# A CIN kernel: chunk 0 in single tiles, W1 in two loads, another order for V and R, and chunk 5's fields behind the stores

## What is computed

```python
X0 = inputs.reshape(-1, 32, 64); Xi = X0; pools = []
for W, b in ((W1, b1), (W2, b2), (W3, b3)):
    Wr = W.reshape(128, 32, Xi.shape[1])
    Xi = jnp.einsum('bhd,bmd,ohm->bod', X0, Xi, Wr) + b[None, :, None]
    pools.append(Xi.sum(axis=-1))
return jnp.concatenate(pools, axis=-1) @ fc_W.T + fc_b
```

## Time and profile before

| what | value |
|---|---|
| three runs | 77.54, 78.10, 78.97 us, median 78.1 |
| the profiled execution | 78.03 us, span 76.2 us, granted TensorE clock 1.00 |
| busy of the span | TensorE 92%, VectorE 66%, ScalarE 49%, GpSimd 46% |
| DMA | 14.10 MB, mean 185 GB/s |

### The profile page before, as it was taken

How to read it: one execution, slowest core, us unless ns; L and a number is a source line. 1 busy time by engine, 2 the same in 40 slices (tenths; PEclk the granted TensorE clock), 3 DMA queues, 4 the chain that set the end, 5 groups by cost and what they waited for, 6 DMA issues and landing times.

```text
span 76.2 us, 1113 instructions
## 1 busy us (share of the span) xinstructions
PE 69.8 (92%) x353; PEld 48.7 (64%) x353; DVE 50.1 (66%) x53; ACT 37.7 (49%) x57; POOL 35.1 (46%) x40
## 2 busy tenths in 40 slices
PE   3999279999899999879999999999999999999970
PEld 1335057666432588568887888888888888877750
DVE  1035999997489888999968497999691300303541
ACT  3720895999799999915767229600760021000000
POOL 4924164992488401910001920999999530053200
DMA  0899999999999999345149997000000000000000
GB/s 11 237 302 241 364 374 361 350 371 388 391 430 386 431 402 354 122 124 154 32 133 421 389 307 297 17 0 0 0 0 0 4 0 0 9 0 0 0 0 0
DMA packets 7337, 14.10 MB, mean 185 GB/s; under 512 B 771, under 2 KB 3907, under 8 KB 6819
## 3 DMA queue, kind: packets, MB, share of 16 engines
q1 hardware_dynamic: 6995, 13.78, 51.3%
q10 hardware_dynamic: 336, 0.25, 1.2%
HBM read 12.98 MB, written 1.05 MB: 184 GB/s over the span
## 4 chain that ended last, share of the span: by engine, by line
PE 72%; ACT 12%; DVE 10%; issue 3%; DVEq 0%
PE a_ps L627 29%; PE x_ps L627 21%; PE x_ps L611 5%; ACT feat L351 5%; PE z_ps L621 4%; ACT zz L351 3%; PE a_ps L713 3%; ACT x L365 3%; PE a_ps L689 2%; PE a_ps L688 2%; DVE z_ps L477 2%; PE x_ps L662 2%; ACT at_sb L351 2%; DVE feat L484 2%; DVE products_of L477 2%
## 5 line engine op out<-in xcount | busy, mean ns | idle before, releaser
L627 PE MATMUL x_ps<-feat,w_hi 128*128 128x512 f32 x64 | 19.3, 402 | 2.7 <-ACT feat L351 1.8
L268 POOL TENSOR_TENSOR xs<-x_in,xs 32x512 fp32r<-32x512 f32 x7 | 9.0, 1285 | 15.9 <-ACT xs L351 14.6
L351 ACT ACTIVATE feat<-z_ps 128x1024 fp32r<-128x1024 f32 x12 | 12.0, 1019 | 8.4 <-POOL xsum L338 5.0
L627 PE MATMUL a_ps<-feat,a_hi 128*128 128x512 f32 x64 | 16.1, 394 | 0.0
L627 PEld LDWEIGHTS x_ps<-feat,w_hi 128*128 128x128 f32 x64 | 11.5, 189 | 6.6 <-issue 3.3
L627 PEld LDWEIGHTS a_ps<-feat,a_hi 128*128 128x128 f32 x64 | 12.0, 188 | 2.8
L275 POOL TENSOR_TENSOR feat<-products_of,feat 128x1024 fp32r<-128x1024 f32 x4 | 9.5, 2387 | 7.9 <-DVE z_ps L477 4.7
L527 DVE SCALAR_TENSOR_TENSOR x<-a_ps,vec,x 128x512 f32<-128x512 f32 x7 | 5.2, 748 | 11.3 <-PE a_ps L689 11.3
L282 POOL TENSOR_TENSOR x<-x 128x512 f32<-128x512 f32 x6 | 7.8, 1292 | 8.1 <-DVE x L527 7.8
L477 DVE TENSOR_TENSOR z_ps<-x_in,r_in 128x1024 f32<-128x1024 f32 x8 | 10.8, 1380 | 0.4 <-DVE products_of L477 0.2
L484 DVE TENSOR_TENSOR feat<-z_ps,feat 128x1024 fp32r<-128x1024 f32 x8 | 9.7, 1222 | 1.7 <-ACT feat L351 1.6
(11 more groups left out here) (69 smaller groups left out, 69.7 us busy)
## 6 DMA issues: line engine op xcount, KB each, us to landing
w_sb<-w SPq DMA_DIRECT2D x9, 512.0 KB, 8.8
r_in<-xr SPq DMA_DIRECT2D x4, 1024.0 KB, 11.5
x_in<-xl SPq DMA_DIRECT2D x8, 256.0 KB, 6.1
a_by_fields<-at_sb SPq DMA_DIRECT2D x4, 192.0 KB, 4.2
x<-x_pairs SPq DMA_DIRECT2D x1, 512.0 KB, 6.5
x<-x SPq DMA_DIRECT2D x1, 512.0 KB, 5.6
w_sb<-w SPq DMA_DIRECT2D x1, 256.0 KB, 6.8
a_by_fields<-at_sb SPq DMA_DIRECT2D x2, 128.0 KB, 4.5
```

The costliest lines, as they stand in the source:

```text
L268: nc.gpsimd.tensor_tensor(xs[rows, c, :], x_in[rows, c % X_BUFS, :], xs[rows, c, :].bitcast(f32), ALU.subtract).then_inc(xs_lo, 1)
L351: return nc.scalar.activation(dst, src, ACT.Copy)
L627: nc.tensor.matmul(bank, weights[:, k, :], feat[:, c, part, k, :], start=(start and k == 0), stop=False)
```

## The change

- SP: W1's four main tiles come in two loads, `w1_first_in` and `w1_in`, with `load_x(1)` between; W1's rest is loaded before `x_pairs`; the right fields of chunk 5 are issued behind the six stores, not ahead of them.
- GpSimd sums W1's main tiles in two halves. ScalarE rounds them in two halves (`main_hi`), and rounds the rest earlier.
- Chunk 0, half 0: `first_mult` multiplies tile by tile, `first_hi_parts` rounds tile by tile.
- VectorE: W1's low part stands behind `lo(0)` and W1's rest sum; `pairs_lo(0)` to `(3)` come earlier; of A, `main_lo` stands ahead of the rest's sum.
- TensorE: other order of `pick_right`, layer 1's pieces, V's parts and R's rounds: V in two stretches (two parts each, as before, at other places), R in two stretches with `x1_lo(1, 1)` between.
- ScalarE: other order of `hi`, `save_a`, `save_x1`, `pairs_hi` and the copy of q.

The diff (blank lines and part of the indentation left out):

```diff
@@ -133,6 +133,7 @@
+w1_first_in = sem("w1_first_in")
@@ -140,6 +141,7 @@
+first_picked, first_z, first_hi = sem("first_picked"), sem("first_z"), sem("first_hi")
@@ -211,11 +213,12 @@
-    sp.dma_start(w1_sb[:, :, 0:TILES, :], w1[:, :, 0:TILES, :]).then_inc(w1_in, 16)
+    sp.dma_start(w1_sb[:, :, 0:PER_HALF, :], w1[:, :, 0:PER_HALF, :]).then_inc(w1_first_in, 16)
 ...
+    sp.dma_start(w1_sb[:, :, PER_HALF:TILES, :], w1[:, :, PER_HALF:TILES, :]).then_inc(w1_in, 16)
 ...
+    sp.dma_start(w1_sb[:, :, EVEN:, :], w1[:, :, EVEN:, :]).then_inc(w1_rest_in, 16)
 ...
-    sp.dma_start(w1_sb[:, :, EVEN:, :], w1[:, :, EVEN:, :]).then_inc(w1_rest_in, 16)
@@ -228,13 +231,13 @@
     load_right(PICKED)
     load_x(4)
     load_x(5)
-    load_right(PICKED + 1)
     sp.dma_start(fcb_sb[:, :], fc_b).then_inc(fcb_in, 16)
     for t in range(0, ROUNDS, 2):
         sp.wait_ge(a_saved, t + 2)
         store_a(EXT, 0, t, 0)
         store_a(EXT, 1, t, HALF)
         store_a(H, 0, t, H)
+    load_right(PICKED + 1)
     load_x(6)
     sp.wait_ge(zeros_done, ZEROS)
     sp.wait_ge(a_out, A_OUT)
@@ -301,11 +304,12 @@
-    pool.wait_ge(w1_in, 16)
-    nc.gpsimd.tensor_tensor(w1_sb[:, 0, 0:TILES, :], w1_sb[:, 0, 0:TILES, :], w1_sb[:, 1, 0:TILES, :],
-                            ALU.add).then_inc(w_sum, 1)
+    for half, landed in enumerate((w1_first_in, w1_in)):
+        pool.wait_ge(landed, 16)
+        nc.gpsimd.tensor_tensor(w1_sb[:, 0, of_half(half), :], w1_sb[:, 0, of_half(half), :],
+                                w1_sb[:, 1, of_half(half), :], ALU.add).then_inc(w_sum, 1)
 ...
-    pool.wait_ge(w_sum, 1)
+    pool.wait_ge(w_sum, 2)
@@ -360,6 +364,14 @@
+    def first_hi_parts(k):
+        if k == 0:
+            act.wait_ge(first_z, 1)
+        else:
+            act.wait_ge(z_done, 1)
+        copy(feat[:, 0, 0, k, :], field_bank(0, 0)[:, k, :]).then_inc(first_hi if k == 0 else hi_done, 1)
@@ -368,6 +380,11 @@
+    def main_hi(half):
+        act.wait_ge(w_sum, half + 1)
+        copy(w1_hi[:, of_half(half), :], w1_sb[:, 0, of_half(half), :]).then_inc(w_hi_done, 1)
@@ -379,23 +396,25 @@
     shifted = bass.AP(pick32[:, :].tensor, 0, [list(pick32[:, :].ap[0]), [1, TILES], [TILES, J], [1, H]])
     copy(pick[:, :, :].rearrange("p k (j h) -> p k j h", j=J), shifted).then_inc(pick_done, 1)
     split_x(0)
-    act.wait_ge(w_sum, 1)
-    copy(w1_hi[:, 0:TILES, :], w1_sb[:, 0, 0:TILES, :]).then_inc(w_hi_done, 1)
-    hi(0, 0)
+    first_hi_parts(0)
     split_x(1)
+    first_hi_parts(1)
+    main_hi(0)
+    split_x(2)
+    main_hi(1)
     hi(0, 1)
-    split_x(2)
     act.wait_ge(z16_done, 1)
     copy(z16_hi[:, :], x16[:, 0, :]).then_inc(hi16_done, 1)
     pairs_hi(0, 0)
+    pairs_hi(0, 1)
     hi(1, 0)
-    pairs_hi(0, 1)
+    hi(1, 1)
+    act.wait_ge(w_rest_sum, 1)
+    copy(w1_hi[:, EVEN:, :], w1_sb[:, 0, EVEN:, :]).then_inc(w_hi_done, 1)
     split_x(3)
     pairs_hi(1, 0)
-    hi(1, 1)
     pairs_hi(1, 1)
-    act.wait_ge(w_rest_sum, 1)
-    copy(w1_hi[:, EVEN:, :], w1_sb[:, 0, EVEN:, :]).then_inc(w_hi_done, 1)
+    hi(2, 0)
     act.wait_ge(vt_ready, 1)
     copy(vt_sb[:, :], vt_ps).then_inc(vt_saved, 1)
     act.wait_ge(v_ready, 1)
@@ -404,26 +423,27 @@
     copy(v_st[:, 0:H].rearrange("o (g c) -> o g c", g=4), v_by_field).then_inc(v_saved, 1)
     copy(v_st[:, H:H + 8], v_by_field[:, 0, :]).then_inc(v_saved, 1)
     copy(v_st[:, H + 8:H + 15], v_by_field[:, 1, 0:7]).then_inc(v_saved, 1)
+    hi(2, 1)
     act.wait_ge(vec_in, 16)
+    save_x1(0)
+    hi(3, 0)
+    save_a(0)
+    save_a(1)
     act.wait_ge(v_saved, 1)
     copy(v_rep[:, :, :], v_st[:, 0:H].rearrange("o (h r) -> o h r", r=1).to_broadcast(
         [P, H, 4])).then_inc(v_saved, 1)
-    hi(2, 0)
-    hi(2, 1)
-    save_a(0)
-    hi(3, 0)
-    save_a(1)
-    save_x1(0)
+    hi(3, 1)
     save_a(2)
     pairs_hi(2, 0)
     save_a(3)
+    save_x1(1)
     pairs_hi(2, 1)
     pairs_hi(3, 0)
-    save_x1(1)
-    hi(3, 1)
+    pairs_hi(3, 1)
+    act.wait_ge(q_ready, 1)
+    copy(q_sb[:, :], q_ps).then_inc(q_saved, 1)
     hi(4, 0)
     hi(4, 1)
-    pairs_hi(3, 1)
     save_x1(2)
     act.wait_ge(zeros_done, ZEROS)
     act.wait_ge(a_out, A_OUT)
@@ -434,18 +454,16 @@
     hi(5, 0)
     save_x1(3)
     hi(5, 1)
+    save_x1(4)
     act.wait_ge(f_sum, 1)
     copy(a_hi[:, 0:TILES, :], f1[:, 0:TILES, :]).then_inc(a_hi_done, 1)
-    save_x1(4)
-    act.wait_ge(q_ready, 1)
-    copy(q_sb[:, :], q_ps).then_inc(q_saved, 1)
     act.wait_ge(f_sum, 2)
     copy(a_hi[0:TERMS, TILES:, :], f1[0:TERMS, TILES:, :]).then_inc(a_hi_done, 1)
     split_x(4)
     split_x(5)
-    save_x1(5)
     hi(6, 0)
     split_x(6)
+    save_x1(5)
     hi(6, 1)
     split_x(7)
     hi(7, 0)
@@ -480,6 +498,8 @@
+        if c == 0:
+            dve.wait_ge(first_hi, 1)
@@ -527,18 +547,28 @@
+    def first_mult():
+        for k in range(PER_HALF):
+            if k == 0:
+                dve.wait_ge(first_picked, 1)
+            else:
+                dve.wait_ge(picked, 1)
+            nc.vector.tensor_tensor(field_bank(0, 0)[:, k, :], x_in[:, 0, :], field_bank(0, 0)[:, k, :],
+                                    ALU.mult).then_inc(first_z if k == 0 else z_done, 1)
 ...
-    mult(0, 0)
+    first_mult()
 ...
-    dve.wait_ge(w_hi_done, 1)
-    main_lo(w1_sb[:, 0, :, :], w1_hi, w1_lo, w_lo_done)
 ...
+    dve.wait_ge(w_hi_done, 2)
+    main_lo(w1_sb[:, 0, :, :], w1_hi, w1_lo, w_lo_done)
@@ -546,32 +576,32 @@
     lo(1)
     mult(2, 0)
     mult(2, 1)
-    dve.wait_ge(w_hi_done, 2)
+    pairs_lo(0)
+    dve.wait_ge(w_hi_done, 3)
     rest_lo(w1_sb[:, 0, :, :], w1_hi, w_lo_done)
-    pairs_lo(0)
+    lo(2)
     mult(3, 0)
+    mult(3, 1)
     pairs_lo(1)
-    lo(2)
+    pairs_lo(2)
     lo(3)
-    pairs_lo(2)
-    mult(3, 1)
+    pairs_lo(3)
     mult(4, 0)
     mult(4, 1)
     lo(4)
     second_lo(4)
     mult(5, 0)
-    pairs_lo(3)
     mult(5, 1)
     lo(5)
     dve.wait_ge(f_main_in, F_MAIN)
     nc.vector.tensor_tensor(f1[:, 0:TILES, :], f1[:, 0:TILES, :], f2[:, 0:TILES, :], ALU.add).then_inc(f_sum, 1)
     second_lo(5)
+    dve.wait_ge(f_sum, 1)
+    dve.wait_ge(a_hi_done, 1)
+    main_lo(f1, a_hi, a_lo, a_lo_done)
     dve.wait_ge(f_rest_in, F_REST)
     nc.vector.tensor_tensor(f1[0:TERMS, EVEN:LIN, :], f1[0:TERMS, EVEN:LIN, :], f2[0:TERMS, EVEN:, :],
                             ALU.add).then_inc(f_sum, 1)
-    dve.wait_ge(f_sum, 1)
-    dve.wait_ge(a_hi_done, 1)
-    main_lo(f1, a_hi, a_lo, a_lo_done)
     dve.wait_ge(f_sum, 2)
     dve.wait_ge(a_hi_done, 2)
     rest_lo(f1, a_hi, a_lo_done)
@@ -620,6 +650,8 @@
+            if c == 0 and half == 0 and k == 0:
+                last.then_inc(first_picked, 1)
@@ -631,7 +663,9 @@
-        pe.wait_ge(w_hi_done, 1)
+        pe.wait_ge(w_hi_done, half + 1)
+        if c == 0 and half == 0:
+            pe.wait_ge(first_hi, 1)
@@ -657,7 +691,7 @@
-        pe.wait_ge(w_hi_done, 2)
+        pe.wait_ge(w_hi_done, 3)
@@ -720,59 +754,51 @@
     pick_right(0, 0)
     pick_right(0, 1)
     keep_clock(5)
-    x1_hi(0, 0)
-    x1_main(0, 1)
+    x1_main(0, 0)
     pick_right(1, 0)
-    x1_low_weights(0, 1)
+    pick_right(1, 1)
+    x1_low_weights(0, 0)
+    x1_hi(0, 1)
     x1_lo(0, 0)
-    pick_right(1, 1)
     v_part(0)
     v_part(1)
-    x1_main(1, 0)
     pick_right(2, 0)
-    x1_low_weights(1, 0)
+    x1_hi(1, 0)
     pick_right(2, 1)
+    x1_lo(1, 0)
+    x1_lo(0, 1)
     v_part(2)
     v_part(3)
-    x1_lo(1, 0)
-    x1_main(1, 1)
+    pick_right(3, 0)
+    x1_tail(0)
     pe.wait_ge(ident_done, 2)
     pe.wait_ge(vt_saved, 1)
     nc.tensor.transpose(v_ps, vt_sb[:, :], ident[:, :]).then_inc(v_ready, 1)
-    x1_lo(0, 1)
-    x1_tail(0)
-    pick_right(3, 0)
+    x1_hi(1, 1)
+    pick_right(3, 1)
     a_round(0)
-    x1_low_weights(1, 1)
     a_round(1)
+    x1_lo(1, 1)
     a_round(2)
     a_round(3)
-    pick_right(3, 1)
-    x1_lo(1, 1)
     x1_tail(1)
-    x1_main(2, 0)
-    x1_low_weights(2, 0)
+    x1_hi(2, 0)
     x1_lo(2, 0)
-    x1_main(2, 1)
-    x1_low_weights(2, 1)
-    x1_main(3, 0)
-    x1_low_weights(3, 0)
-    x1_lo(2, 1)
-    x1_tail(2)
+    x1_hi(2, 1)
     pe.wait_ge(v_saved, 4)
     pe.wait_ge(a_saved, ROUNDS)
     nc.tensor.matmul(q_ps, v_rep[:, :, :].rearrange("p h r -> p (h r)"), vec[:, 1:2],
                      start=True, stop=True).then_inc(q_ready, 1)
+    x1_hi(3, 0)
+    x1_lo(2, 1)
+    x1_tail(2)
     x1_lo(3, 0)
-    x1_main(3, 1)
-    x1_main(4, 0)
-    x1_low_weights(4, 0)
-    x1_low_weights(3, 1)
+    x1_hi(3, 1)
+    x1_hi(4, 0)
+    x1_lo(4, 0)
     x1_lo(3, 1)
-    x1_lo(4, 0)
-    x1_main(4, 1)
     x1_tail(3)
-    x1_low_weights(4, 1)
+    x1_hi(4, 1)
     x1_lo(4, 1)
     x1_tail(4)
     x1_hi(5, 0)
```

## The result

The change makes the kernel slower: 80.09 us (median of four executions, 79.59 to 81.86) against 78.03 us, ratio 1.026 with the interval [1.016, 1.037]: it is slower, while whether by more than 2% is open. The profiled execution took 79.79 us, span 78.0. I had forecast 76.6. Executions more than 1.5% above the fastest of the same kernel are left out of every ratio and interval.

A forecast was written before the change was run, and what follows sets the result against it. TensorE, unbroken from 39.30 to 72.70 us, was bound by the A product's start; 1.28 us earlier plus the 0.24 us stall gave 1.5 us together, so 76.6 us against the 78.1 median, range 75.6 to 78.3.

The forecast's parts named there:

- S: Time at which chunk 5's fields land, when `mult(5,0)` can start: forecast 32.7 us, issue at 27.8 plus about 4.9.
- the rival "slower": Chunk 5's fields land late; at 8.2 us latency the A product starts at 40.95: 79.4 us, chance 0.12.
- The formula from S: Chain from the landing of chunk 5's fields through `lo(5)`, `f_sum` and `a_hi`: A product 4.95 us after the landing.
- 1.5 us: Whole forecast gain: 1.28 us from an earlier A product, plus the 0.24 us stall removed.
- 38.05: Forecast start in us of chunk 0's A product, 39.33 before: 1.28 us gained.
- the 0.24 us stall: TensorE's wait before `a_lo` inside the A product, forecast to vanish because `main_lo` now precedes the late `f_rest` sum.
- the last reloads of A: Reloads ahead of the A product, forecast to land by 35.3 us, before `f_sum` at 36.2.
- the collision: At the front, GpSimd's `split_x(1)` overlapping VectorE's `rest_sum`: a 0.15 us slip would cost 0.6 us.
- a wall: W3's last quarter, landing at 17.0 us before V's last two parts: nothing at the front moves V by more than 0.3 us.
- the front's 0.76 us: First feature matmul on TensorE at 8.9 us in place of 9.66: 0.76 gained, not kept whole.

The follow-up runs named there:

- fields ahead of the stores: Changed kernel with chunk 5's fields issued right behind the fourth `save_a`, ahead of the last three stores: ratio 1.026 to the kernel before, median 80.13 us.
- fields alone: Changed kernel with `load_x(6)` behind the reloads of A, and both queues waiting for chunk 5's fields before issuing reloads: 80.23 us, read for the landing only.
- the fields back: Changed kernel with chunk 5's fields issued at their old place, ahead of the stores: ratio 1.004 to the kernel before, median 78.57 us.
- the last run: Changed kernel with chunk 5's fields in halves, first A product's last two matmuls later, `save_x1(3)` before `hi(5, 0)`, `load_x(6)` behind reloads: ratio 0.992, median 77.34 us.
- the run with the fields between the stores: Changed kernel with chunk 5's fields issued behind the first three stores and ahead of the last three: ratio 1.042 to the kernel before, median 81.0 us.

## Why the prediction was wrong

**The step that failed** is the landing of chunk 5's fields: "The nearest row is chunk 6's fields, 4.9 us from issue to landing on a short queue: 32.7 us." The issue came as forecast (27.91, forecast 27.8), the landing took 7.84 us, and S was 35.75, not 32.7. The place, the wait and the point from which it decides (S above 34.4) stood in the rival "slower", whose 8.2 us and 79.4 us come near the 7.84 and 80.09 measured; I gave it 0.12, because I took a queue that has run out for a fast queue. The rates around it show the opposite (windows view of the kernel after; last two columns: DMA share, GB/s):

```profile
29.00:30.00 1.00, 1.00 (x6) 0.83 (x5) 0.44 (x1) 0.97 (x3) 0.48 (x1) 1.00 0.74 156
30.00:31.00 1.00, 1.00 (x6) 0.82 (x5) 0.69 (x1) 1.00 (x2) 1.00 (x1) 1.00 0.71 205
...
32.00:33.00 1.00, 1.00 (x5) 0.82 (x6) 0.66 (x1) 0.00 (x0) 0.00 (x0) 1.00 0.95 379
```

From 29 to 31 us the DMA engines are busy for 0.7 of the time and move 156 and 205 GB/s. The single packets of the trace, those of 8 KB, in which the fields come:

```
kernel, load               packets   first begins    first packets take     then
before, chunk 5 (full)       128     behind chunk 4  0.31 to 0.34 us        0.31 us
before, chunk 6              128     38.96 us        0.87 to 1.01 (five)    mostly 0.31 us
after, chunk 5               128     29.15 us        0.47 to 1.48 (17)      mostly 0.31 us
fields ahead of the stores   128     27.32 us        1.43 to 1.62 (eight)   mostly 0.31 us
```

A load that is issued when little is left in the queue begins 1.0 to 1.3 us after its issue, and its first packets take up to five times as long as the rest. A load that stands behind others in a full queue has no slow packets, and its start is hidden. Chunk 6's fields in the kernel before have both; their 4.9 us contain it. The three parts of a landing, with what else went through the DMA engines meanwhile, from the same packets:

```
kernel, load               to the first  first packet to  to the    other data
                           packet        end of the last  landing   meanwhile
before, chunk 6            1.15 us       3.36 us          0.4 us    0.12 MB
fields alone, chunk 5      1.30 us       4.63 us          0.4 us    0.03 MB
after, chunk 5             1.24 us       5.86 us          0.7 us    0.56 MB
```

The wait ahead of the first packet is about the same in all three. What grew is the middle: by 1.3 us with nothing behind the load, and by as much again with `load_x(6)` and the reloads in the same engines. What single packets took beyond 0.31 us comes to 0.7 us per DMA engine in the last two rows and 0.2 in the first, a part of the growth only. Why the first packets are slower behind the stores, these runs don't show.

**The formula from S.** "The A product is at S+4.95": it came 5.46 us behind the landing (35.75 to 41.21). From the first product of chunk 5 it was 5.4 us, 5.6 with the fields back and 5.95 in the last run: `save_x1(3)` stands between `hi(5, 0)` and layer 1 of chunk 5, and `f_sum` came 3.6 to 4.3 us after that product where I had 3.5. Together the two errors give the start of the A product: 3.05+0.5 us over 37.65 (32.7+4.95) are 41.2.

**The bound behind it.** Had the fields landed as forecast, there would still have been no 1.5 us. In the last run nothing waited for them, no stall was left inside the A product, and it started at 38.80, not at 38.05: 0.53 us ahead of the earlier trace rows and the 0.24 us stall make 0.8, and 0.6 us were measured. With the fields back it started at 38.45, and the last reloads of A, which I had on time, took the gain again with their 1.78 us.

**What was right.** The stations up to 32 us lie within about 0.6 us: first feature matmul 8.78 (8.9), `rest_sum` 0.42 us and not 1.00, low weights 10.85 (10.8), `vt_sb` 18.37 (18.1), first round 21.00 (20.6), chunk 1's tail 25.40 (25.1), last `save_a` 25.81 (25.7), stores over at 30.28 (30.3), `x1_hi(4, 0)` 31.86 (31.25). `split_x(1)` did run just ahead of `rest_sum`, so the collision that I weighed with the Trainium skill (SBUF — State Buffer, "Who interferes with whom") didn't arise; `pairs_lo(3)` took 1.51 us at 25.16 while GpSimd's `lo(2)` ran from 23.25 to 26.13, as that rule has it, and was covered.

**The wall at the front.** I called W3's last quarter a wall. It landed at 17.3 us, and TensorE came to the part that needs it, the second of the stretch that began at 17.22, 0.4 us later: it bound nothing. The second quarter did. It stands in the chain that ended last (5.62 to 13.53), the second V part starts at 13.57, and in the traces of four runs `vt_sb` follows that start by 4.8 us, whether the first feature matmul was at 8.30, 8.78 or 9.16. I had the V parts from 12.65 to 13.85 without a wait and `vt_sb` at 18.1; it came at 18.37. And the row that the front's 0.76 us were counted from, 9.66, was that of an execution with a late W1.

## What to carry to other kernels

A large load moved to the end of a queue is not priced by its bytes: look whether the queue has run dry by then, add the slow start, and bound it by what shares the queue behind it, above all when the compute engines need it at a fixed time. Halve such a load where its user takes it in halves; that kept most of the stores' gain and cut the wait from 3.17 us to 0.55 and 1.02 in two traces. When a chain of stores and reloads is moved, follow its last small load as closely as its main one. And before a station of one trace is taken for the kernel's, look at a second: here the same front order began 0.75 us earlier where one load had landed 1.0 us earlier.

## What the runs showed of the hardware that I had not expected

- The slow start of a load in a queue that has nearly run dry: first packets of 8 KB 0.5 to 1.6 us (up to 2.1 in the run with the fields between the stores), later ones mostly 0.31; 1 MB took 4.9 to 8.9 us from issue to landing in six kernels. In a full queue none of its packets took over 0.34 us, at 354 to 431 GB/s.
- The same load in the same order of loads landed after 6.5, 7.0 and 7.5 us in three traces of the changed kernel's order (half 1, 0.5 MB), as late as other runs' 1 MB.
- TensorE's clock after a wait near the middle of the kernel: behind holes of 2.1 to 3.4 us the granted clock fell in some executions and not in others (0.60 on average over 4 us in the run with the fields between the stores, 1.00 in the profiled execution of the changed kernel). A hole can cost more than its length: the changed kernel took 81.86 us in the execution with a mean clock of 0.979, and 79.59 to 80.38 in the others.
